# Cross-attention and mixture of experts: weighted sums of eight heads at a time, the projection in two halves

## The chip, the cores and the metric

One core of a Trainium2 chip. The time is that of one execution of the kernel on the device, in microseconds; less is better. Three runs of the kernel before took 1474.66, 1475.11 and 1478.47 us, median 1475.11 us.

## What is computed

The input is `x` of 32 batches of 112 tokens with 256 channels, and a context of 32 x 375 rows with 192 channels. One layer of cross-attention with 16 heads of 64, then a layer of 8 experts of which each token takes 2:

```python
q = (x @ Wq).reshape(b, lq, H, DK).transpose(0, 2, 1, 3)           # x after a layernorm
kv = (y @ Wkv).reshape(b, lkv, 2, H, DK).transpose(2, 0, 3, 1, 4)
atten = softmax(einsum('bhid,bhjd->bhij', q, k) * SCALE)
out = einsum('bhij,bhjd->bhid', atten, v) ... @ Wproj + bproj       # x = x + out
hidden = silu(gate_out) * up_out                                    # x after a second layernorm
output = sum of the two chosen experts' hidden @ down_w, by their gate shares   # x = x + output
```

## The kernel before, in words

Everything is one program in which each engine has its own list of instructions, written out by hand, and semaphores between them. TensorE (PE), VectorE (DVE), ScalarE (ACT), GpSimd (POOL) and SyncE (SP) each go through their list in order. First comes attention, then the experts (63 tiles of 128 rows). The change is in attention.

Attention runs in **pairs** of batches (`pair(i)`, 16 of them, `odd` = 0 and 1 within a pair), each batch in four **steps** (`s` = 0 to 3) of four heads. In a step PE does, in this order:

- the scores of four heads into the four PSUM banks `S_ps` (`scores`, L1521);
- products for the batch ahead: two blocks of K, begun by a short pair of 64-row products (`tails`, L1493, then `context_product`, L1486);
- an item "early" from the table `ahead`: a q product (L1429) or the transposes of `xn` (L1447);
- transposes of the probabilities of two heads (`turn_prob`, L1531), a V product (L1486), an item "mid", transposes of the other two heads, a second V product, an item "late";
- the weighted sums of the step's four heads into `O_ps` (`weigh`, L1555), and the tails of the two V products (L1493).

In step 2 there are no V products. There the projection of the batch before (`project`, L1576, 24 matmuls into `A_ps[1]`) stands between the K products and the transposes, and the small products that count tokens per expert (`count`, L1585) before the weighted sums.

Around it, ACT takes the exponentials (L891), the high parts of K, q and xT out of PSUM (L847 to L851), the transposed probabilities of heads 2 and 3 (`turned`, L897), at the end of step 0 four sums over the experts' gate products (`sum_experts`, L903), and one V block (L845). DVE takes the row maxima (`most`, L1279), the low parts (L1046), the transposed probabilities of heads 0 and 1 (L1285), the residual and its mean and variance (`residual`, L1125 to L1132, in step 2), the ranks of tokens in experts (`assign`, L1199 to L1207, in step 2) and the other V block (L1036). POOL normalises x2 (`norm_h`, L745 to L753) and splits the attention's result for the projection (`split_O`, L710).

A V block and a K block can share a bank: V's half 1, tile 1 (made in step 0, taken out by ACT at the step's end) lies in `A_ps[0]`, and so does the first K block of step 1. PE waits for a bank in `free_bank`, before the tails of K:

```python
for k in of_K:
    free_bank(a, k)
...
tails(a, of_K, True)
```

The last pair (`i == NP - 1`) is written out apart. Its gate logits go over PE: `turn_hn` (L1593) transposes the normalised rows of the batch before, which needs POOL's `hn`.

Of the kernel before, what the change touches and what calls it, by code (L numbers as in the profile page):

```python
# [65 lines left out]
PLACES = ("K", "early", "mid", "V", "late")  # L66


def ahead(odd, s):

    q_at = {(1, 0): (0,), (1, 1): (1,), (1, 2): (2, 3), (1, 3): (4,), (0, 0): (5,), (0, 1): (6,), (0, 2): (7,)}.get((odd, s), ())
    one = [("q", p) for p in q_at] + {(0, 2): [("xT", 0)], (0, 3): [("xT", 1)]}.get((odd, s), [])
    places = {"K": [("K", 2 * s), ("K", 2 * s + 1)],
              "early": one if s < 2 else [],
              "mid": one[:1] if s >= 2 else [],
              "V": [("V", t) for t in {0: ((1, 1), (1, 2)), 1: ((0, 0), (0, 1)), 3: ((0, 2), (1, 0))}.get(s, ())],
              "late": one[1:] if s >= 2 else []}
    return [(odd, s, place, kind, a) for place in PLACES for kind, a in places[place]]  # L80

# [20 lines left out]
def bank_of(items, k):  # L102
# [7 lines left out]
    return {"early": 1, "mid": 0 if s == 2 else 7, "late": 1}[place]  # L110
# [90 lines left out]

def dram_at(t, b):

    return t[b] if known(b) else t[bass.ds(b, 1)].rearrange("o q c -> (o q) c")


def attention_and_experts(nc, x, ctx_in, Wq, Wkv, Wproj, bproj, gate_w, gate_up_w, down_w, out):
# [4 lines left out]
    with ExitStack() as stack:  # L212
# [40 lines left out]
        gw_rows = nc.alloc_sbuf_tensor_at("gw_rows", [LQ, C, E], F32, offset=wgu_at + E * C * 4)  # L253
        weighed = nc.alloc_sbuf_tensor_at("weighed", [LQ, 2, C], F32, offset=wgu_at + E * C * 4)
        multiplied = nc.alloc_sbuf_tensor_at("multiplied", [LQ, E // 2, C], F32, offset=wgu_at + E * C * 4 + 2 * C * 4)
        logits = nc.alloc_sbuf_tensor_at("logits", [LQ, E], F32, offset=wgu_at + E * C * 4 + (2 + E // 2) * C * 4)
        assert 2 * E * C * 4 <= shared_from - wgu_at
# [14 lines left out]
        probT = sb("probT", [KR, 4, KT * LQ], F32)  # L272
# [57 lines left out]
        early = 2  # L330
        place["at"] = wd_at + early * FJ * C * 4
# [135 lines left out]
        def _(sp):  # L467
# [65 lines left out]
            def pair(i):  # L533
                a = Ahead(i)
                if known(i) and i == NP - 2:
                    sp.dma_start(Wd[:, 0:early].rearrange("p e k n -> p (e k) n"),
                                 down_w[0:early].rearrange("e (k p) n -> p (e k) n", p=P)).then_inc(wd_early, 16)
                for odd in (0, 1):
# [17 lines left out]
                    if known(i) and i == NP - 1 and not odd:  # L556
                        sp.wait_ge(gates_done, B - 3)
                        load_expert(sp, 0)
                    if known(i) and i == NP - 1 and odd:
# [274 lines left out]
        def _(act):  # L834
# [59 lines left out]
            def turned(b, s, j):  # L894

                act.wait_ge(probT_made, H * b + 4 * s + j + 1)
                nc.scalar.copy(probT[:, j, :], S_ps[j][0:KR, 0:KT * LQ]).then_inc(probT_second, 1)  # L897
# [19 lines left out]
            def pair(i):  # L917
                a = Ahead(i) if there(i, NP) else None
                for odd in (0, 1):
                    b = 2 * i + odd  # L920
                    for s in range(NS):
# [20 lines left out]
                        if there(b, B):  # L942
                            turned(b, s, 2)
                            turned(b, s, 3)
                        if s == 0 and there(b - 2, B) and by_vector(b - 2):
                            sum_experts(b - 2)
                        for k in made_at["late"]:
                            evacuate(a, k)
# [67 lines left out]
        def _(dve):  # L1016
# [102 lines left out]
            def residual(i, b, slot, bank):  # L1119
# [5 lines left out]
                nc.vector.tensor_tensor(x2[:, slot, :], bank[0:LQ, 0:C], x_bias[:, slot, :], ALU.add).then_inc(x2_done, 1)  # L1125
                dve.wait_ge(x2_done, b + 1)
# [155 lines left out]
            def turned(b, s, j):  # L1282

                dve.wait_ge(probT_made, H * b + 4 * s + j + 1)
                nc.vector.tensor_copy(probT[:, j, :], S_ps[j][0:KR, 0:KT * LQ]).then_inc(probT_first, 1)  # L1285

            def pair(i):
                a = Ahead(i) if there(i, NP) else None
                for odd in (0, 1):
                    b = 2 * i + odd  # L1290
                    for s in range(NS):
# [7 lines left out]
                        if s == 3 and there(b - 1, B) and not by_vector(b - 1):  # L1299
                            keep_hnT(b - 1, A_ps[1])  # L1300
# [480 lines left out]
```

## Time and profile before

| what | value |
|---|---|
| median of 3 runs | 1475.11 us |
| the profiled execution | 1475.41 us, of which its span 1473.6 us |
| PE busy | 1432.4 us (97%) |
| DVE, ACT, POOL busy | 1058.9 us (72%), 856.5 us (58%), 624.7 us (42%) |
| granted TensorE clock, mean | 0.992 |
| first scores of the first batch | 30.71 us |
| first scores of the last step | 1126.27 us |

Times in rows are counted from the first instruction. A PE row's duration is a modelled one with the latency in it; how long PE is held by a group is read from the start of one group to the start of the next. "Idle before" names what an engine waited for. In the order of instructions, register and ISA rows carry no work.

### The profile page before, as it was taken

The numbers are of one execution on the slowest core, as the hardware profiler recorded it, in microseconds if no ns is written. First come the engines' busy times: TensorE is split into PE (matmuls) and PEld (weight loads), VectorE is DVE, ScalarE is ACT, GpSimd is POOL, SyncE is SP. The second block draws the span as 40 slices with busy tenths as digits, with TensorE's granted clock in tenths as the row PEclk, the third lists the DMA queues.
The fourth block names the chain that finished last, engine by engine and source line by source line (L and its number), as shares of the span: only waits on it lengthen the run. The fifth ranks groups of instructions, "written<-read, shape, count | busy, mean of one in ns | idle before, by whom it ended". The sixth has DMA issues, their size and how long they took to land.

```text
span 1473.6 us, 38599 instructions
## 1 busy us (share of the span) xinstructions
PE 1432.4 (97%) x11960; PEld 1266.3 (86%) x11961; DVE 1058.9 (72%) x2868; ACT 856.5 (58%) x2392; POOL 624.7 (42%) x671
## 2 busy tenths in 40 slices
PE   6999999999999999999999999999997999999996
PEld 5888888888888888888888888888886788888885
DVE  5667777777777777777777777777768776666664
ACT  5566556555665566656655655556655555555553
POOL 2634344344545343545344443545436242333332
PEclk9999999999999999999999999999998899999998
DMA  9322222222222222322222222212128233333332
GB/s 262 108 68 69 75 73 74 67 76 67 73 67 73 73 80 78 94 82 68 73 67 73 74 73 70 73 38 73 28 64 314 50 66 56 55 52 57 51 57 26
DMA packets 101508, 114.75 MB, mean 78 GB/s; under 512 B 17276, under 2 KB 88172, under 8 KB 101356
## 3 DMA queue, kind: packets, MB, share of 16 engines
q1 hardware_dynamic: 88300, 95.25, 22.0%
q0 software_dynamic: 12144, 15.66, 5.9%
q10 hardware_dynamic: 1024, 3.34, 0.7%
q8 instruction: 21, 0.34, 0.1%
q14 instruction: 19, 0.16, 0.0%
HBM read 62.28 MB, written 51.93 MB: 78 GB/s over the span
## 4 chain that ended last, share of the span: by engine, by line
PE 87%; DVE 6%; DMA 3%; issue 2%; ACT 2%; DVEq 0%; ACTq 0%; POOLq 0%; SPq 0%
PE bank L1486 23%; PE bank L1429 22%; PE bank L1555 11%; PE bank L1531 10%; PE bank L1521 8%; PE bank L1576 6%; PE bank L1493 4%; DVE neg_max L1279 2%; DMA out<-y_out,dest_now 2%; PE bank L1731 2%; ACT prob L891 1%; DVE probT L1285 1%; PE bank L1684 1%; DVE Wgu L1138 1%; DMA WkU_whole<-in_L_xattn_Wkv 0%
## 5 line engine op out<-in xcount | busy, mean ns | idle before, releaser
L891 ACT ACTIVATE prob<-bank,neg_max 112x375 f32<-112x375 f32 x512 | 299.0, 589 | 133.7 <-DVE neg_max L1279 133.7
L1279 DVE TENSOR_REDUCE neg_max<-bank 112x1 f32<-112x375 f32 x512 | 244.0, 540 | 14.5 <-PE bank L1521 14.4
L1531 PE MATMUL bank<-ident,prob 112*125 112x112 f32 x1536 | 216.5, 273 | 6.5 <-ACT prob L891 2.4
L1531 PEld LDWEIGHTS bank<-ident,prob 112*125 112x125 f32 x1536 | 197.7, 188 | 20.0 <-ACT prob L891 14.0
L822 POOL DMA_INDIRECT out<-y_out,dest_now x63 | 97.8, 1553 | 200.4 <-DMA out<-y_out,dest_now 144.4
L1555 PEld LDWEIGHTS bank<-probT,V 125*64 125x64 f32 x3072 | 149.1, 137 | 39.0 <-issue 36.5
L1046 DVE TENSOR_TENSOR K_l<-bank,K_h 128x376 fp32r<-128x376 f32 x256 | 140.5, 550 | 56.9 <-ACT K_h L847 52.7
L1555 PE MATMUL bank<-probT,V 125*64 125x112 f32 x3072 | 176.6, 264 | 2.7 <-DVE probT L1285 1.9
L1429 PE MATMUL bank<-Wgu,hT_h 128*128 x504 | 166.6, 412 | 2.3 <-DVE hT_l L1347 2.2
L845 ACT COPY V<-bank 125x512 f32<-125x512 f32 x96 | 56.5, 588 | 164.3 <-PE bank L1493 161.7
L847 ACT CAST K_h<-bank 128x376 fp32r<-128x376 f32 x256 | 121.0, 473 | 31.7 <-PE bank L1486 29.4
L710 POOL CAST OT_h<-O_now 128x448 fp32r<-128x448 f32 x64 | 37.5, 586 | 213.1 <-DVE O_now L1115 213.1
L745 POOL TENSOR_SCALAR std<-mv 112x1 f32<-112x1 f32 x32 | 7.7, 240 | 281.9 <-DVE mv L1132 281.9
L1285 DVE COPY probT<-bank 125x336 f32<-125x336 f32 x256 | 121.3, 495 | 0.1
L897 ACT COPY probT<-bank 125x336 f32<-125x336 f32 x256 | 100.3, 443 | 27.4 <-PE bank L1531 27.0
L1486 PE MATMUL bank<-yA_h,WkH 128*128 128x376 f32 x256 | 99.6, 389 | 12.3 <-DVE WkU L1064 12.3
L1036 DVE COPY V<-bank 125x512 f32<-125x512 f32 x96 | 66.4, 692 | 62.0 <-PE bank L1493 55.5
L1429 PEld LDWEIGHTS bank<-Wgu,hT_h 128*128 128x128 f32 x504 | 91.0, 191 | 22.4 <-issue 5.3
L1008 ACT ACTIVATE y_out<-bank,share_now 128x256 f32<-128x256 f32 x63 | 29.9, 475 | 137.4 <-PE bank L1429 137.4
L891 ACT ACTIVATION_READ_ACCUMULATOR prob<-bank,neg_max 112x1 f32 x512 | 108.1, 211 | 0.0
L1429 PE MATMUL bank<-Wgu,hT_l 128*128 x252 | 100.1, 397 | 0.0
L849 ACT CAST q_h<-bank 128x224 fp32r<-128x224 f32 x128 | 45.4, 355 | 85.6 <-PE bank L1429 85.6
(217 smaller groups left out, 4008.9 us busy)
## 6 DMA issues: line engine op xcount, KB each, us to landing
bins<-pad_rows SPq DMA_DIRECT2D x29, 1032.0 KB, 5.9
inv_rows<-sums SPq DMA_DIRECT2D x126, 128.0 KB, 2.9
h_in<-bins SPq DMA_DIRECT2D x63, 129.0 KB, 2.3
Wgu<-in_L_ffn_gate_up_w SPq DMA_DIRECT2D x6, 1024.0 KB, 7.0
y_sb<-in_ctx SPq DMA_DIRECT2D x32, 187.5 KB, 2.7
y_sb<-in_ctx SPq DMA_DIRECT2D x62, 93.8 KB, 2.7
x_sb<-in_x SPq DMA_DIRECT2D x16, 224.0 KB, 3.0
x_res<-in_x SPq DMA_DIRECT2D x32, 112.0 KB, 2.4
```

Source lines behind the costliest of these rows:

```text
L822: pool.indirect_dma_start(out, bass.IndirectOffsetOnAxis(ap=dest_now[:, (k + 3) % 4:(k + 3) % 4 + 1], axis=0), y_out[:, (k + 1) % 2, :], N ...
L847: nc.scalar.copy(K_h[:, arg, :], src[:, 0:LKE]).then_inc(hi_done, 1)
L891: nc.scalar.activation(prob[:, j, :], S_ps[j][0:LQ, 0:LKV], ACT.Exp, bias=neg_max[:, j:j + 1], accum_out=row_sum[:, head // HB, head % HB: ...
L897: nc.scalar.copy(probT[:, j, :], S_ps[j][0:KR, 0:KT * LQ]).then_inc(probT_second, 1)
L1046: nc.vector.tensor_tensor(lo, ps, hi.bitcast(F32), ALU.subtract).then_inc(lo_done, 1)
L1279: nc.vector.tensor_reduce(neg_max[:, j:j + 1], S_ps[j][0:LQ, 0:LKV], AX.X, ALU.max, negate=True).then_inc(max_done, 1)
L1285: nc.vector.tensor_copy(probT[:, j, :], S_ps[j][0:KR, 0:KT * LQ]).then_inc(probT_first, 1)
L1429: last = mm(dst, w, m, start=n == 0, stop=n == len(todo) - 1)
L1486: last = mm(out, w, y, start=begins and n == 0, stop=ends and n == "both")
L1521: last = mm(S_ps[2 * k + r][0:LQ, 0:LKE], w[rows, p, q], m[rows, p, :], start=n == 0, stop=n == len(todo) - 1)
L1531: last = nc.tensor.transpose(S_ps[j][0:KR, t * LQ:t * LQ + LQ], prob[:, j, t * KR:t * KR + KR], ident[0:LQ, 0:LQ])
L1555: last = mm(O_ps[r * DK:r * DK + DK, c:c + LQ], V[:, t, (2 * p + r) * DK:(2 * p + r) * DK + DK], probT[:, 2 * k + r, t * LQ:t * LQ + LQ], ...
```

## The change

- `weigh` runs only at the end of steps 1 and 3, for eight heads, in all pairs but the last (`merged`). The transposed probabilities of even and odd steps go to two tiles; `probT_odd` lies where four small tiles were, which move to the room of the first experts' down weights, and those weights' load moves into the last pair.
- Scores of steps 1 and 3 get waits of their own for the transposed probabilities to be out of `S_ps`.
- The projection's first half stays before the first transposes of step 2, the second half goes behind the second transposes.
- `residual` loses its mean and variance, which go to step 3 behind the low parts of K (`moments`); the residual itself goes behind the transposed probabilities and the item "mid".
- The place "late" goes away. Items: q0 and q1 in step 0 of the odd batch, q2 in its step 1, q3 in step 2 (mid), q4 in step 3 (early), q5 and q6 in step 0 of the even batch, q7 in its step 1; xT of step 2 in "mid", of step 3 in "early".
- In the last pair `turn_hn` stands behind the second transposes of step 3.

```diff
-    q_at = {(1, 0): (0,), (1, 1): (1,), (1, 2): (2, 3), (1, 3): (4,), (0, 0): (5,), (0, 1): (6,), (0, 2): (7,)}.get((odd, s), ())
+    q_at = {(1, 0): (0, 1), (1, 1): (2,), (1, 2): (3,), (1, 3): (4,), (0, 0): (5, 6), (0, 1): (7,)}.get((odd, s), ())
...
+def merged(i):
+
+    return not known(i) or i < NP - 1
...
                     if known(i) and i == NP - 1 and not odd:
                         sp.wait_ge(gates_done, B - 3)
+                        sp.wait_ge(pv_made, NS * (B - 2))
                         load_expert(sp, 0)
+                        sp.dma_start(Wd[:, 0:early].rearrange("p e k n -> p (e k) n"),
...
-            def turned(b, s, j):
+            def turned(b, s, j, to):
...
                 nc.vector.tensor_tensor(x2[:, slot, :], bank[0:LQ, 0:C], x_bias[:, slot, :], ALU.add).then_inc(x2_done, 1)
+
+            def moments(b, slot):
+
                 dve.wait_ge(x2_done, b + 1)
                 nc.vector.bn_stats(stat2[:], x2[:, slot, :]).then_inc(st2, 1)
...
+                        if s == 3 and there(b - 1, B):
+                            moments(b - 1, 1 - odd)
                         if s == 2 and there(b, B):
                             normalise(b, 0)
-                        if s == 2 and there(b - 1, B):
-                            residual(i, b - 1, 1 - odd, A_ps[1])
...
                         for k in made_at["mid"]:
                             low_part(a, k)
+                        if s == 2 and there(b - 1, B):
+                            residual(i, b - 1, 1 - odd, A_ps[1])
...
+                    if s % 2 and merged(b // 2 if known(b) else b):
+                        pe.wait_ge(probT_second if k else probT_first, 2 * NS * b + 2 * s)
...
-                            project(b - 1, A_ps[1])
-                        if s == 3 and there(b - 1, B) and not by_vector(b - 1):
-                            for k in a.at(odd, 2, "late") if a else []:
-                                pe.wait_ge(lo_done, a.split(k))
-                            turn_hn(b - 1, 1 - odd, A_ps[1])
+                            project(b - 1, A_ps[1], (0,))
...
                             turn_prob(b, s, 1)
+                        if s == 2 and there(b - 1, B):
+                            project(b - 1, A_ps[1], (1,))
+                        if s == 3 and there(b - 1, B) and not by_vector(b - 1):
+                            turn_hn(b - 1, 1 - odd, A_ps[1])
...
-                        if there(b, B):
-                            weigh(a, odd, s, b)
+                        if there(b, B) and not merged(i):
+                            weigh(a, odd, s, b, probT[0])
+                        if there(b, B) and merged(i) and s % 2:
+                            weigh(a, odd, s - 1, b, probT[0])
+                            weigh(a, odd, s, b, probT[1])
```

How it moves instructions, at three places. PE at the end of step 1, even batch of the repeated pair (L1555 and L1568 are the weighted sums, the rows with `WvU,yT` the tails of V); before, then changed:

```order
L1486 MATMUL bank<-WvL,yA_h 125x512
L1486 MATMUL bank<-WvT,yB 125x512
L1551 REGISTER_ALU
L1555 MATMUL bank<-probT,V 64x112 x12
L1493 MATMUL bank<-WvU,yT 125x512 x2
```

```order
L1497 MATMUL bank<-WvT,yB 125x512
L1552 REGISTER_ALU
L1556 REGISTER_ALU
L1568 MATMUL bank<-probT,V 64x112 x12
L1564 REGISTER_ALU
L1568 MATMUL bank<-probT_odd,V 64x112 x12
L1504 MATMUL bank<-WvU,yT 125x512 x2
```

Two groups of twelve now stand together, and the end of step 0 has none.

ACT in step 0 of the same batch, from the K blocks' high parts on; before, then changed:

```order
L849 CAST q_h<-bank 128x224
L890 REGISTER_ALU
L891 ACTIVATE prob,row_sum<-bank,neg_max 112x375
L897 COPY probT<-bank 125x336 x2
L901 REGISTER_ALU
L903 ACTIVATE multiplied,logits<-multiplied 112x256 x4
L841 REGISTER_ALU
L845 COPY V<-bank 125x512
```

```order
L856 CAST q_h<-bank 128x224
L897 REGISTER_ALU
L898 ACTIVATE prob,row_sum<-bank,neg_max 112x375
L848 REGISTER_ALU
L856 CAST q_h<-bank 128x224
L904 COPY probT<-bank 125x336 x2
L908 REGISTER_ALU
L910 ACTIVATE multiplied,logits<-multiplied 112x256 x4
L848 REGISTER_ALU
L852 COPY V<-bank 125x512
```

A second q block is taken out ahead of the transposed probabilities; the four sums and the V block keep their order behind them.

DVE in step 2 of the same batch, from the low parts of K on; before, then changed:

```order
L1115 TENSOR_TENSOR O_now<-bank,inv_rows 128x448
L1124 REGISTER_ALU
L1125 TENSOR_TENSOR x_115<-bank,x_bias 112x256
L1127 BN_STATS stat_117<-x_115 112x6
L1132 BN_AGGR mv_118<-stat_117 112x2
L1285 COPY probT<-bank 125x336 x2
L1038 REGISTER_ALU
L1046 TENSOR_TENSOR q_l<-bank,q_h 128x224
L1038 REGISTER_ALU
L1046 TENSOR_TENSOR xT_l<-bank,xT_h 128x2x112
L1199 TENSOR_TENSOR bin_at<-bank,running 112x8
```

```order
L1121 TENSOR_TENSOR O_now<-bank,inv_rows 128x448
L1294 COPY probT<-bank 125x336 x2
L1044 REGISTER_ALU
L1052 TENSOR_TENSOR xT_l<-bank,xT_h 128x2x112
L1130 REGISTER_ALU
L1131 TENSOR_TENSOR x_112<-bank,x_bias 112x256
L1208 TENSOR_TENSOR bin_at<-bank,running 112x8
L1210 TENSOR_TENSOR running<-bank,running 128x8
L1211 TENSOR_TENSOR picked<-onehot,bin_at 112x16
```

The residual now stands between the last low part and the ranks, directly ahead of step 3's maxima.

## Rows read from the trace of the kernel before

**Rows 1.** One pair (us; PE, PEld, DVE, ACT, POOL busy; clock; DMA share; GB/s).

```profile
653.76:723.16 69.40, 69.09 (x630) 61.32 (x628) 52.22 (x155) 41.73 (x130) 31.34 (x36) 1.00 0.24 74
```

**Rows 2.** PE timeline, step 0 into 1 (start, duration, engine, line, out<-in, count).

```profile
658.78 0.81 PE L1531 MATMUL bank<-ident,prob 112*125 112x112 f32 x6
659.36 0.48 PE L1486 MATMUL bank<-WvH,yA_h 128*125 128x512 f32 x1
660.45 1.37 PE L1555 MATMUL bank<-probT,V 125*64 125x112 f32 x24
661.75 0.49 PE L1493 MATMUL bank<-WvU,yT 64*125 64x512 f32 x2
663.10 0.35 PE L1493 MATMUL bank<-yT,WkU 64*128 64x376 f32 x2
```

**Rows 3.** Chain of waits from 600 us on: a piece of one weighted-sum group.

```profile
599.99 0.77 PE bank L1555 x16
```

**Rows 4.** ACT timeline, end of the same step 0.

```profile
661.48 0.20 ACT L903 ACTIVATION_READ_ACCUMULATOR multiplied<-multiplied 112x1 f32 x1
662.28 0.59 ACT L845 COPY V<-bank 125x512 f32<-125x512 f32 x1 [0.61 <-PE bank L1493]
```

**Rows 5.** One transpose after a wait (timeline); the group's mean (page).

```profile
648.43 0.36 PE L1531 MATMUL bank<-ident,prob 112*125 112x112 f32 x1
L1531 PE MATMUL bank<-ident,prob 112*125 112x112 f32 x1536 | 216.5, 273 | 6.5 <-ACT prob L891 2.4
```

**Rows 6.** PE timeline, step 3 of the same batch.

```profile
679.72 0.42 PE L1521 MATMUL bank<-K_h,q_h 64*112 64x376 f32 x2
682.57 1.20 PE L1531 MATMUL bank<-ident,prob 112*125 112x112 f32 x6
683.53 0.47 PE L1486 MATMUL bank<-WvH,yA_h 128*125 128x512 f32 x1
```

**Rows 7.** DVE timeline, end of step 2 into step 3.

```profile
676.31 0.42 DVE L1125 TENSOR_TENSOR x<-bank,x_bias 112x256 f32<-112x256 f32 x1 [1.09 <-PE bank L1576]
676.76 0.43 DVE L1127 BATCH_NORM_STATS2 stat<-x 112x6 f32<-112x256 f32 x1
679.23 0.16 DVE L1199 TENSOR_TENSOR bin_at<-bank,running 112x8 f32<-112x8 f32 x1
680.51 1.91 DVE L1279 TENSOR_REDUCE neg_max<-bank 112x1 f32<-112x375 f32 x4 [0.45 <-PE bank L1521]
683.53 0.55 DVE L1046 TENSOR_TENSOR K_l<-bank,K_h 128x376 fp32r<-128x376 f32 x1 [0.38 <-ACT K_h L847]
```

**Rows 8.** PE timeline, end of step 2: token counts, then the weighted sums.

```profile
678.18 0.17 PE L1585 MATMUL bank<-chosen,before 112*112 112x8 bf16 x1
678.41 1.18 PE L1555 MATMUL bank<-probT,V 125*64 125x112 f32 x20
```

**Rows 9.** ACT timeline, step 3.

```profile
681.10 0.58 ACT L891 ACTIVATE prob<-bank,neg_max 112x375 f32<-112x375 f32 x1 [2.21 <-DVE neg_max L1279]
682.09 0.47 ACT L847 CAST K_h<-bank 128x376 fp32r<-128x376 f32 x1 [0.33 <-PE bank L1486]
682.46 0.58 ACT L891 ACTIVATE prob<-bank,neg_max 112x375 f32<-112x375 f32 x1
```

**Rows 10.** POOL timeline, the normalised rows of that batch.

```profile
678.84 2.44 POOL L753 TENSOR_SCALAR hn<-x,mv,std 112x256 f32<-112x256 f32 x2 [0.20 <-POOL std L747]
```

**Rows 11.** Last step of all, PE and DVE timelines.

```profile
1126.27 0.43 PE L1521 MATMUL bank<-K_h,q_h 64*112 64x376 f32 x2
1131.52 2.51 PE L1555 MATMUL bank<-probT,V 125*64 125x112 f32 x24
1127.14 1.91 DVE L1279 TENSOR_REDUCE neg_max<-bank 112x1 f32<-112x375 f32 x4
```

**Rows 12.** Busy time by stretch, last pair.

```profile
1096.23:1126.27 30.04, 26.50 (x257) 22.65 (x256) 20.25 (x58) 18.29 (x47) 23.31 (x18) 1.00 0.55 188
1131.30:1138.00 6.70, 6.30 (x42) 5.49 (x40) 5.93 (x11) 2.16 (x3) 2.85 (x2) 0.50 1.03 407
```

More of the change, by code:

```diff
@@ L58 @@
 N2 = NT - N1
-PLACES = ("K", "early", "mid", "V", "late")
+PLACES = ("K", "early", "mid", "V")
 def ahead(odd, s):
-    q_at = {(1, 0): (0,), (1, 1): (1,), (1, 2): (2, 3), (1, 3): (4,), (0, 0): (5,), (0, 1): (6,), (0, 2): (7,)}.get((odd, s), ())
-    one = [("q", p) for p in q_at] + {(0, 2): [("xT", 0)], (0, 3): [("xT", 1)]}.get((odd, s), [])
+    q_at = {(1, 0): (0, 1), (1, 1): (2,), (1, 2): (3,), (1, 3): (4,), (0, 0): (5, 6), (0, 1): (7,)}.get((odd, s), ())
+    ones = [("q", p) for p in q_at] + {(0, 2): [("xT", 0)], (0, 3): [("xT", 1)]}.get((odd, s), [])
     places = {"K": [("K", 2 * s), ("K", 2 * s + 1)],
[L76 to L79, printed above, removed]
+              "early": ones[:1] if s != 2 else [],
+              "mid": ones[1:] if s != 2 else ones,
+              "V": [("V", t) for t in {0: ((1, 1), (1, 2)), 1: ((0, 0), (0, 1)), 3: ((0, 2), (1, 0))}.get(s, ())]}
     return [(odd, s, place, kind, a) for place in PLACES for kind, a in places[place]]
@@ L109, in bank_of @@
         return int(a in SECOND)
-    return {"early": 1, "mid": 0 if s == 2 else 7, "late": 1}[place]
+    return {"early": 1, "mid": 0 if s == 2 else 7}[place]
 class Ahead:
@@ L330, in attention_and_experts @@
         early = 2
+        gw_rows = nc.alloc_sbuf_tensor_at("gw_rows", [LQ, C, E], F32, offset=wd_at)
+        place["at"] = wd_at
+        weighed = sb("weighed", [LQ, 2, C], F32)
+        multiplied = sb("multiplied", [LQ, E // 2, C], F32)
+        logits = sb("logits", [LQ, E], F32)
+        assert place["at"] <= wd_at + early * FJ * C * 4 and E <= early * FJ
         place["at"] = wd_at + early * FJ * C * 4
@@ L942, in pair @@
                         if there(b, B):
-                            turned(b, s, 2)
-                            turned(b, s, 3)
+                            to = probT[s % 2 if merged(i) else 0]
+                            turned(b, s, 2, to)
+                            turned(b, s, 3, to)
                         if s == 0 and there(b - 2, B) and by_vector(b - 2):
                             sum_experts(b - 2)
-                        for k in made_at["late"]:
-                            evacuate(a, k)
                         if known(b) and b == B - 1 and s == 3:
@@ L1533, in turn_prob, with weigh @@
                     last.then_inc(probT_made, 1)
-            def weigh(a, odd, s, b):
+            def weigh(a, odd, s, b, weights):
                 if s == 0:
@@ L1556, in weigh @@
                                       V[:, t, (2 * p + r) * DK:(2 * p + r) * DK + DK],
-                                      probT[:, 2 * k + r, t * LQ:t * LQ + LQ], start=t == 0, stop=t == KT - 1)
+                                      weights[:, 2 * k + r, t * LQ:t * LQ + LQ], start=t == 0, stop=t == KT - 1)
                 last.then_inc(pv_made, 1)
@@ L1566, in turn_last_inverses, with project @@
                 last.then_inc(inv_turned, 1)
-            def project(b, bank):
+            def project(b, bank, halves=range(2)):
                 if known(b) and b == 0:
                     pe.wait_ge(wp_done, 8)
-                for half in range(2):
+                for half in halves:
                     pe.wait_ge(OT_lo, 2 * b + half + 1)
@@ L1577, in project @@
                                       stop=j == NJ - 1 and n == 2)
-                last.then_inc(proj_made, 1)
+                if 1 in halves:
+                    last.then_inc(proj_made, 1)
             def count(b):
@@ L1625, in pair @@
                         for k in early:
+                            if s == 3 and there(b - 1, B):
+                                pe.wait_ge(x2_done, b)
                             make(a, k, i)
@@ L1645, in pair @@
                             turn_prob(b, s, 1)
+                        if s == 2 and there(b - 1, B):
+                            project(b - 1, A_ps[1], (1,))
+                        if s == 3 and there(b - 1, B) and not by_vector(b - 1):
+                            turn_hn(b - 1, 1 - odd, A_ps[1])
                         for k in of_V[1:]:
@@ L1652, in pair @@
                             context_product(a, k, True, False)
-                        for k in made_at["late"]:
-                            if there(b - 1, B):
-                                pe.wait_ge(x2_done, b)
-                            make(a, k, i)
                         if s == 0 and there(b - 2, B) and not by_vector(b - 2):
```

33 lines of the change are left out of this document (13 added, 20 removed).

## Prediction

> **What bounds the kernel now.** I read the busy shares first: PE is busy 97% of the span. So the second view is one pair by itself, and there PE is busy 69.09 of 69.40 us at a granted clock of 1.00 [rows 1]. A pair costs what PE's list costs, plus the few places where PE waits. That made the PE timeline the third view: where is an interval from one group to the next longer than the same group's elsewhere? Then the timelines of DVE and ACT around those places, and those of the last pair. Only three kinds of terms can matter: PE time that the new order saves, waits that go, and waits that come. 14 pairs are alike; the first and the last are counted apart.
>
> **Weighted sums merged.** A group of 24 PE instructions holds PE from 660.45 to 661.75, 1.30 us [rows 2]. Inside a group 16 of them take 0.77 us [rows 3], so 24 alone would take 1.155. The other 0.145 us is paid at the group's edges, where PE changes from one division of its array to another. The change joins 8 groups of a pair into 4: 4 x 0.145 = **0.58 us saved a pair**. Other edges stay: V's tails (64 rows) follow a 128-row product instead of the sums, which is a change of division too.
>
> **Step 2's end.** In the even batch the counts stand at 678.18 and the sums start at 678.41 [rows 8], 0.23 us for two matmuls that together hold PE about 0.12; the sums waited for DVE's transposed probabilities. They are no longer there to wait: **0.12 saved**. The new waits of the scores of steps 1 and 3 cost nothing: between the last transposes and the second pair of scores lie V product and tails (1.09 + 0.33 us) or the projection's second half (about 1.4), and ACT needs 0.5 + 2 x 0.35. Without that cover each would cost up to 1 us.
>
> **Step 1, a new wait.** In step 0 ACT goes through transposed probabilities, four expert sums, then the V block. From the second transposes at 658.78 the last sum is read out at 661.48, 2.70 us later [rows 4]. The V copy now starts only at 662.28 because it waits for V's tails, lands 0.59 us later, and PE needs its bank at 663.10, for the K tails of step 1 [rows 2, 4]: a margin of 0.2 us. In the change 1.30 us of weighted sums is gone from between. PE comes to the K tails 663.10 - 658.78 - 1.30 = 3.02 us after the transposes. ACT is no faster: the copy can start at 2.70 + 0.1, lands at 3.39, and is seen a few hundredths later. The second q product stands ahead of the transposes and moves both alike. **PE waits about 0.41 us**, and the first matmul after a wait shows 0.36 against a mean of 0.273 [rows 5], 0.09 more. That is 0.5 us a batch, **1.0 a pair**. DVE is late here as well (its count of the top gates waits for the same sums, and V copy and maxima stand behind it: some 0.8 us), but PE stands still 0.5 of that and ACT's wait for the K products takes up the rest.
>
> The Trainium skill (TensorE: Matmul & The Clock Gate, "Step-by-step: what each phase is for") says that TensorE pulls weight loads ahead of matmuls in flight. By that a restart would cost nothing, and the sum would be 4 x 0.09 a pair, some 5 us in all, lower. The trace sides with the cost: the lone transpose above. I keep 0.09.
>
> **Step 3, the old wait.** Transposes begin at 682.57 and the V product at 683.53, 0.96 us [rows 6], against 0.58 in step 0 [rows 2]: PE waits 0.38 us for the second head's exponentials, in each batch. The change puts a q product (0.66 us, as in step 0) ahead of them in the odd batch and two xT transposes (0.19) in the even one. But DVE now comes later. Its maxima start 0.79 us after the scores (679.72 to 680.51), waiting only for PE. In the change the residual waits for the projection's second half, directly before the scores: it starts some 0.2 us after them (a matmul's latency of 0.3 less the counts' 0.1, an estimate), then 0.45 to the ranks (676.31 to 676.76), then 0.83 (679.23 to 680.51 less 0.45 idle) [rows 7]. So the maxima start about 1.45 us in, 0.65 later. ACT takes up most of it, since it idled 0.33 before the first K copy [rows 9]: the second exponential, now 2.74 us in, comes at 2.85 to 2.95. The odd batch is covered at the first transposes; at the second, with the q copy in ACT's list before the last exponential, about 0.1 us is left: 0.38 becomes 0.1, **0.28 saved**. The even batch has 0.19 us of cover against 0.38 plus 0.15, and 0.2 to 0.3 at the second transposes (the xT copy now stands before the last exponential): 0.38 becomes 0.55, **0.17 lost**.
>
> **What costs nothing.** Mean and variance move to step 3: DVE is busy 52 of 69 us [rows 1], and the work behind them (transposed probabilities) has the sums of step 2's heads as cover, 1.2 us. POOL's norm starts some 4 us later; it is busy 31 of 69 us. If that cover were gone, the gate products would delay DVE's V copy at the next step 0. Later O_now in step 0, later split: the projection is 10 us away. The loads of down weights queue on SP behind expert 0 and are wanted after attention. Without cover that would be up to 6 us, once.
>
> **A pair:** -0.58 - 0.12 + 1.0 + 0.17 - 0.28 = **+0.19 us**; 14 of them +2.7. The first pair has no expert sums, so no wait in step 1: -0.8.
>
> **The last pair.** It keeps groups of four heads, so it saves no edges. (a) Batch 30, step 3: `turn_hn` needs POOL's rows. Mean and variance now follow the second low part of K, which starts at 3.8 us in (683.53 - 679.72) and takes about 0.5. From their start to the first half of `hn` it is 678.84 - 676.76 = 2.1, plus half of 2.44 [rows 7, 10]: ready at about 7.7 us. PE arrives at 5.5 (scores 1.1, K 1.7, transposes 0.96, V 1.0, transposes 0.6). It waits 2.2 us, and the V product then waits 0.6 for DVE to copy the result; with more at the transposes: +3.2. (b) In step 2 of batches 30 and 31 the second half projection covers what PE waited for: -1.3. (c) Last step: the maxima start 0.87 us in [rows 11]. Residual, ranks and the five steps of the plan (2.4 us) follow the projection, from which the scores are only 1.3 us of sums away: maxima at about 1.75. Then mean and variance, 3.3 us to `hn`, transposes, copy, and the inverse sums behind them on DVE: the weighted sums start about 9 us in, against 1131.52 - 1126.27 = 5.25 [rows 11]. +3.7, and what follows up to the first experts hangs on it. Together **+5.6 us**.
>
> **Sum:** 2.7 - 0.8 + 5.6 = +7.5 us. The profiled execution was 1475.4 us (span 1473.6), as good as the median of 1475.1. **Forecast: 1483 us.**
>
> **Bounds.** The wait in step 1, by the copy's own margin, is at least 0.3 and, if the read-out must end first, 0.6 with restart and late DVE 0.8: -0.4 to +0.6 a pair, -6 to +8 us. A 128-row product directly before V's tails is not in the rows inside a pair; its edge could be nothing or the 0.145: -0.3 to +0.3 a pair. The last pair: 2 (PE busy elsewhere hides half) to 8.
>
> **Rivals.** (1) *Waits outweigh the edges mildly*, the forecast: 1479.5 to 1487. For it: the margin of 0.2 us in step 1 against 1.3 removed. Chance 0.60. (2) *ACT is in time.* If the V copy lands before PE is 3.02 us past the transposes, the edges remain: pair -0.8, 15 x -0.8 + 5.6 = -6.4, so **1469**. It decides at a copy done 0.4 us sooner than its row allows. Against it: ACT's four sums run without a gap. Chance 0.09. (3) *The last pair is cheap*: POOL and DVE chains overlap with waits that exist already, +2 rather than +5.6, and the pairs near zero: **1477**, no change. Chance 0.12. (4) *The end turns slow.* The granted clock was 1.00 from 1096 to 1126 us with PE busy 26.5 of 30 us, and 0.50, the 1.2 GHz level, from 1131.3 to 1138.0 after step ends full of waits [rows 12]. More waits begin at batch 30's step 3 already. One more such stretch of 6.7 us at half speed gives away up to 3.4, two about 5, and step-1 waits of 0.6 add 5: **1489**. Chance 0.19.
>
> The Trainium skill (same page, "The HAM clock gate") has TensorE fall back to half rate after idling; by that rule (4) would gain weight. The trace agrees as to the fall at 1131.3, but shows none at the waits of the last pair before.
>
> That the merge does not take place is ruled out by the order of instructions.
>
> **Numbers.** 0.3%, 4.4 us, is about what a measurement can tell from no change. Slower by more: (1) and (4), 0.79. Same: (3), 0.12. Faster: (2), 0.09. The range leaves out (2) and the far end of (4): 1476 to 1491.
>
> **What would show it.** A pair of 69.4 to 69.8 us; groups of 48 instructions of 2.45 us; before the K tails of step 1 a gap of 0.4 us ended by ACT's V copy; transposes of step 3 at 0.58 in the odd and about 0.7 in the even batch; in batch 30 over 2 us of PE waiting for `hn`. The prediction is wrong if step 1 shows no gap, or if the last scores of attention start less than 3 us later than 1126.27.

## The result: slower by 1.0%

| | before | changed |
|---|---|---|
| median of 5 runs each | 1476.74 us | 1492.03 us |
| ratio | | 1.0101 (95% interval 1.0086 to 1.0117) |
| span of the profiled execution | 1473.6 us | 1489.7 us |
| a pair of batches | 69.40 us | 69.90 us |
| from the last pair's first scores to the end | 403.4 us | 412.2 us |

The forecast was 1483.0 us (1476 to 1491): the sign was right, the size half of what came. Of 16.1 us between the two spans, 14 pairs bring 7.0 (forecast 2.7), the last pair and the end 8.7 (forecast 5.6), the first pair -0.3 (forecast -0.8); the rest is a first score 0.7 us later. Two executions, one of the kernel before with 4788.1 us and one of the kernel with pieces (below) with 2751.6 us, are left out of all medians and ratios as slow ones.

The pair that answers to [rows 1], and its first two steps (busy time by stretch; PE, PEld, DVE, ACT, POOL; clock):

```profile
658.16:728.06 69.90, 69.29 (x632) 61.56 (x629) 53.27 (x155) 41.10 (x130) 31.72 (x37) 1.00 0.25 74
658.16:665.85 7.69, 7.69 (x59) 6.76 (x57) 5.78 (x14) 5.84 (x20) 5.72 (x5) 1.00 0.79 239
665.85:675.89 10.04, 9.74 (x102) 8.38 (x100) 7.17 (x28) 5.64 (x20) 5.40 (x9) 1.00 0.16 45
```

Step 0 has no wait. Step 1 has one of 0.30 us in every batch, and it is the one forecast. PE and ACT timelines around it, as in [rows 2, 4]:

```profile
663.83 0.81 PE L1544 MATMUL bank<-ident,prob 112*125 112x112 f32 x6
666.71 0.33 PE L1534 MATMUL bank<-K_h,q_l 64*112 64x376 f32 x2
667.33 0.44 PE L1504 MATMUL bank<-yT,WkU 64*128 64x376 f32 x2 [0.30 <-ACT V L852]
...
666.54 0.19 ACT L910 ACTIVATION_READ_ACCUMULATOR multiplied<-multiplied 112x1 f32 x1
666.63 0.57 ACT L852 COPY V<-bank 125x512 f32<-125x512 f32 x1
```

From the second transposes (663.83) to the last sum's read-out (666.54) it is 2.71 us, as before. The V copy follows at once, lands at 667.20, and PE starts the K tails at 667.33. "Idle 0.30" is less than PE loses, since the modelled ends of the matmuls in flight cover part of it. By starts it is more: over the 12 pairs in the middle, scores and K tails of step 1 take 1.86 us in either batch, where before they took 1.30. That is 0.56 us a batch.

Step 3 of the same even batch, the rows that answer to [rows 6, 7, 9]:

```profile
686.16 1.04 PE L1544 MATMUL bank<-ident,prob 112*125 112x112 f32 x6
687.99 0.94 PE L1544 MATMUL bank<-ident,prob 112*125 112x112 f32 x6
683.27 0.42 DVE L1131 TENSOR_TENSOR x<-bank,x_bias 112x256 f32<-112x256 f32 x1 [1.40 <-PE bank L1589]
684.39 1.91 DVE L1288 TENSOR_REDUCE neg_max<-bank 112x1 f32<-112x375 f32 x4
685.89 0.58 ACT L898 ACTIVATE prob<-bank,neg_max 112x375 f32<-112x375 f32 x1
```

The scores began at 683.10. The residual starts 0.17 us behind them (forecast 0.2), the maxima 1.29 (forecast 1.45), the second exponential 2.79 (forecast 2.85 to 2.95). The first transposes wait 0.23 us, the second 0.38; averaged over the pairs, transposes and V products of this step take 0.26 us more in the even batch and 0.24 less in the odd one.

The last pair. PE timeline of batch 30's step 3, then POOL and DVE around the start of batch 31's step 2:

```profile
1111.03 0.38 PE L1607 MATMUL bank<-ident,hn 112*128 112x112 f32 x2 [2.13 <-POOL hn L760]
1109.65 2.44 POOL L760 TENSOR_SCALAR hn<-x,mv,std 112x256 f32<-112x256 f32 x2 [0.20 <-issue]
1107.56 0.42 DVE L1136 BATCH_NORM_STATS2 stat<-x 112x6 f32<-112x256 f32 x1
...
1127.18 4.57 POOL L699 TENSOR_TENSOR Wgu<-Wgu 128x2048 fp32r<-128x2048 f32 x1
1128.55 3.24 DVE L1188 CAST top_f<-top_i 112x2 f32<-112x2 uint32 x1
```

The 2.13 us for `hn` are the forecast 2.2. The last two rows were not foreseen. DVE's cast of the chosen experts' numbers, two to a row, takes 3.24 us, where its median over the kernel is 0.17, and it ends at 1131.79 us; POOL's subtraction, the low part of an expert's weights, ends at 1131.75. In the kernel before the same pair of rows stands there, but the cast takes only 1.18 us, since POOL's subtraction ended 2 us earlier against the step (0.25 us behind its first scores, now 2.30):

```profile
1113.40 4.53 POOL L692 TENSOR_TENSOR Wgu<-Wgu 128x2048 fp32r<-128x2048 f32 x1
1116.78 1.18 DVE L1179 CAST top_f<-top_i 112x2 f32<-112x2 uint32 x1
```

Behind the cast stand the maxima, the exponentials and PE: step 2 of batch 31 takes 10.64 us, before 8.59. What PE and DVE do there, first the kernel before (its scores at 1117.68), then the changed one (scores at 1129.45):

```profile
1118.56 1.91 DVE L1279 TENSOR_REDUCE neg_max<-bank 112x1 f32<-112x375 f32 x4
1124.97 1.37 PE L1555 MATMUL bank<-probT,V 125*64 125x112 f32 x24 [1.66 <-DVE probT L1285]
```

```profile
1132.38 1.91 DVE L1288 TENSOR_REDUCE neg_max<-bank 112x1 f32<-112x375 f32 x4
1133.67 2.42 PE L1544 MATMUL bank<-ident,prob 112*125 112x112 f32 x12 [1.34 <-ACT prob L898]
```

The wait of 1.66 us ahead of the sums has gone. But the maxima start 2.93 us behind the scores instead of 0.88, so that PE waits ahead of and between the transposes. On top of that the second half projection takes 2.68 us, in batch 30 1.49: the granted clock is 0.50, the 1.2 GHz level, from 1135.6 to 1139.0.

### The profile page after: what moved, and what is told of

The parts are those of the page before. It is cut to its first block and busy times, and to the rows that moved or that the text cites. A ratio compares the mean times of both kernels' runs of the same rounds, so it can differ in the third digit from the quotient of the medians.

```text
span 1489.7 us, 38675 instructions
## 1 busy us (share of the span) xinstructions
PE 1436.0 (96%) x11960; PEld 1270.2 (85%) x11961; DVE 1076.3 (72%) x2868; ACT 847.3 (57%) x2392; POOL 631.4 (42%) x671
## 5 line engine op out<-in xcount | busy, mean ns | idle before, releaser
L1568 PEld LDWEIGHTS bank<-probT,V 125*64 125x64 f32 x1632 | 80.3, 139 | 23.9 <-issue 23.4
L1568 PE MATMUL bank<-probT,V 125*64 125x112 f32 x1632 | 95.1, 267 | 0.0
L1497 PE MATMUL bank<-WvH,yA_h 128*125 128x512 f32 x192 | 91.9, 479 | 0.9 <-DVE hnT L1153 0.6
L1534 PE MATMUL bank<-K_h,q_h 64*112 64x376 f32 x512 | 88.7, 342 | 0.3 <-DVE probT L1294 0.3
L1497 PE MATMUL bank<-yA_l,WkH 128*128 128x376 f32 x256 | 86.4, 337 | 0.0
L1497 PE MATMUL bank<-yB,WkT 128*128 128x376 f32 x256 | 86.2, 337 | 0.0
```

The source lines that it names most:

```text
L1497: last = mm(out, w, y, start=begins and n == 0, stop=ends and n == "both")
L1534: last = mm(S_ps[2 * k + r][0:LQ, 0:LKE], w[rows, p, q], m[rows, p, :], start=n == 0, stop=n == len(todo) - 1)
L1568: last = mm(O_ps[r * DK:r * DK + DK, c:c + LQ], V[:, t, (2 * p + r) * DK:(2 * p + r) * DK + DK], weights[:, 2 * k + r, t * LQ:t * LQ + LQ] ...
```

## The experiments

Twelve runs followed. The first four (the three marked first, and the sums twice) ran in a session in which the kernel before took 1483.9 us instead of 1476.7, so three of them ran once more in a later one, in which it took 1475.2; the record gives the chip the number 2 both times. The ratio is always to the kernel before in the same session. "End" is the time from the last pair's first scores to the end of the span.

| kernel | time | ratio, interval | pair | end |
|---|---|---|---|---|
| the changed kernel again (c_after) | 1492.6 | 1.0112 (1.0097, 1.0127) | 69.89 | 414.4 |
| the kernel before again, one execution (c_before) | 1475.1 | | 69.40 | 402.2 |
| sums early, first (e1) | 1482.4 | 0.999 (0.998, 1.000) | 69.2 | 414.2 |
| sums early, second (c_sums_early) | 1475.6 | 0.9999 (0.9989, 1.0009) | 68.79 | 413.5 |
| sums twice (e2) | 1512.4 | 1.0184 (1.0165, 1.0204) | 72.0 | 407.7 |
| last pair old, first (e3) | 1492.1 | 1.0051 (1.0033, 1.0069) | 70.65 | 403.3 |
| last pair old, second (c_last_pair_old) | 1484.0 | 1.0052 (1.0035, 1.007) | 69.90 | 405.1 |
| unmerged, first (e4) | 1494.6 | 1.0066 (1.0044, 1.0088) | 70.13 | 411.5 |
| unmerged, second (c_unmerged) | 1497.7 | 1.0147 (1.013, 1.0164) | 70.11 | 412.9 |
| moments of the last pair early (e10) | 1486.1 | 1.0064 (1.0047, 1.008) | 69.89 | 406.3 |
| POOL's split in pieces (e8) | 1492.0 | 1.0118 (1.01, 1.0136) | 69.90 | 411.7 |
| both cures (e5) | 1467.9 | 0.9947 (0.9935, 0.9959) | 68.75 | 403.7 |

### Step 1: take the wait away, and make it without the change

Sums early, on the changed kernel, in ACT's step 0:

```diff
+                        if s == 0 and there(b - 2, B) and by_vector(b - 2):
+                            sum_experts(b - 2, 0, 2)
                         for k in made_at["mid"]:
                             evacuate(a, k)
...
-                            sum_experts(b - 2)
+                            sum_experts(b - 2, 2, 4)
```

> The changed kernel, but in step 0 ACT takes two of its four expert sums ahead of the q copy (the item mid) instead of all four at the step's end. Theory (the loss inside a pair is PE's wait at step 1 for ACT's V copy, which stands behind the four sums): the copy comes some 0.8 us sooner, the wait of 0.56 us a batch goes, step 1 falls from 10.04 to about 9.5 us in both batches, a pair from 69.90 to 68.7 to 69.0 us, and the time from 1492.0 by 13 to 17 us to 1475 to 1479. Rival 1 (step 1 is longer since the joined groups change the array's division before V's tails, or since the scores wait for the transposed probabilities): step 1 stays at 10.0 us, the time at 1492. Rival 2 (the two sums ahead of the q copy make that copy and so the last exponentials late): the wait moves to step 0's second transposes, a pair stays at 69.5 or above.

> The changed kernel with two of ACT's four expert sums ahead of the q copy, again, for the same reason. Without the slow handover: step 1 of 9.48, pairs of 68.75, and 1492.0 - 16 = 1476, level with the kernel before (ratio 0.998 to 1.002).

In the second run step 1 took 9.48 us, every pair but the first 68.74 to 68.81, and the time was level with the kernel before. So the wait of step 1 is worth 1.11 us a pair, 15.5 us in all, as much as the whole difference between the two kernels: without it step 1 takes what it took before plus the 1.15 us of the moved sums. ACT has the room: it idled 0.82 us before the second q copy. With both cures the same place reads:

```profile
654.58 0.45 ACT L916 ACTIVATE multiplied<-multiplied 112x256 f32<-112x256 f32 x1
655.54 0.35 ACT L861 CAST q_h<-bank 128x224 fp32r<-128x224 f32 x1
657.55 0.59 ACT L857 COPY V<-bank 125x512 f32<-125x512 f32 x1
...
658.38 0.33 PE L1517 MATMUL bank<-yT,WkU 64*128 64x376 f32 x2
```

The sums stand ahead of the q copy, the V copy starts 0.20 us after PE's scores (657.35), and the tails have no wait and no dearer restart: 0.27 us from their start to the next group's, against 0.37.

Sums twice, on the kernel before, at the end of ACT's step 0:

```diff
+                for e in range(E // 2):
+                    nc.scalar.activation(multiplied[:, e, :], multiplied[:, e, :], ACT.Copy,
+                                         accum_out=logits[:, E // 2 + e:E // 2 + e + 1]).then_inc(more_sums, 1)
+                act.wait_ge(more_sums, 4 * b + 4)
                 for e in range(E // 2):
```

> The kernel before, unmerged, but ACT takes each of the four expert sums twice (four more readings of 0.40 us at the end of step 0, and a wait between the two sets). Nothing else moves. Theory (the V copy behind the sums has a margin of 0.2 us before PE misses its bank, and it idles 0.8 us before it can start): 1.7 us more make the copy 0.9 us later and PE waits 0.7 to 0.9 us before the K tails of step 1 in both batches; step 1 rises from 8.33 to 9.0 to 9.3, a pair from 69.40 to 70.8 to 71.3, the time from 1476.7 by 20 to 28 us. Rival (ACT has room, and what the changed kernel loses in step 1 comes from PE's own order): the pair stays within 0.3 us of 69.40 and the time within 4 us.

```profile
683.85 0.56 ACT L846 COPY V<-bank 125x512 f32<-125x512 f32 x1
684.54 0.43 PE L1498 MATMUL bank<-yT,WkU 64*128 64x376 f32 x2 [0.74 <-ACT V L846]
```

Step 1 rose from 8.33 to 9.33 in both batches, slightly over the forecast. The pair's other 0.56 us, which take it to 72.0 against a forecast of 70.8 to 71.3, stand in step 0 of the odd batch, where the slow handover below stands too. The wait comes with neither merged sums nor a new order, from ACT's list alone, so the rival is gone. What the merge did was to take 1.30 us of PE work from between.

### Is the merge itself worth its edges?

```diff
 def merged(i):
-    return not known(i) or i < NP - 1
+    return False
```

> The changed kernel with the weighted sums at the end of every step, in groups of four heads, in all pairs. All else stays changed. Theory (merging saves 0.60 us a pair at the groups' edges and brings the wait at step 1, 1.13 a pair): steps 0 and 2 rise by 1.30, steps 1 falls to 8.3 to 8.4 and step 3 by 1.15 to 1.2; a pair from 69.90 to 69.2 to 69.6 us, the time falls from 1492.0 by 4 to 10 us, to 1482 to 1488. Rival (the joined groups are worth their edges and the loss in step 1 comes from elsewhere, as the new order of q products): a pair rises by 0.6 to 70.5 and the time to 1500.

> The changed kernel unmerged, again, for the same reason. Without the slow handover, theory: the transposes of step 0 wait 0.2 to 0.3 us (its first run had 0.33, and 0.21 in the last pair, where no slow handover stood), edges cost 0.60, step 1 saves 1.13: pairs of 69.4 to 69.9 us against 69.90, time 1485 to 1492. If step 0 keeps 9.5 and 9.3 us, that wait belongs to the order and not to the chip, and merging is worth more than its edges.

Step 1 fell to 8.33, as the theory has it, and the edges came back (two groups at 1.301 us where one of 48 has 2.451). But the pair rose to 70.13 and 70.11 in the two runs: the transposes of step 0 wait 0.33 us in the even and 0.30 in the odd batch, and the even batch loses 0.18 more behind its second V product. These waits stand in both sessions and belong to the order, then. DVE's timeline shows where it comes from (scores of step 0 at 661.72):

```profile
660.93 0.64 DVE L1163 CUSTOM_DVE_ANT_0 weighed<-hn,gw_wide 112x256 f32<-112x256 f32 x1 [0.22 <-POOL hn L760]
662.89 0.68 DVE L1042 COPY V<-bank 125x512 f32<-125x512 f32 x1
663.49 1.90 DVE L1288 TENSOR_REDUCE neg_max<-bank 112x1 f32<-112x375 f32 x4
```

The gate products wait for POOL's `hn`, late by the mean and variance in step 3, and push V copy and maxima: 1.77 us after the scores, where the kernel before had them at 0.84 (654.60 after 653.76):

```profile
653.99 0.69 DVE L1036 COPY V<-bank 125x512 f32<-125x512 f32 x1
654.60 1.90 DVE L1279 TENSOR_REDUCE neg_max<-bank 112x1 f32<-112x375 f32 x4
```

So my expectation was wrong: in this order the long group at the end of step 3 hides the late `hn`, and merging is worth 0.2 us a pair even with its wait in step 1. (By ratio it is worth 5 to 7 us in all; the pairs account for 3.5 of them, 14 x 0.21 and 0.6 in the first.) The first run's lower ratio (1.0066) says nothing else: there the kernel before was 8.7 us slower and this one 3 us faster than in the second.

### The last pair

Last pair old, on the changed kernel (in `most`; PE's list accordingly: `project` whole, `turn_hn` ahead of the transposes):

```diff
+                        if s == 3 and last_pair(i) and not by_vector(b - 1):
+                            keep_hnT(b - 1, A_ps[1])
...
+                        if s == 2 and last_pair(i):
+                            residual(i, b - 1, 1 - odd, A_ps[1])
+                            moments(b - 1, 1 - odd)
```

> The changed kernel with the last pair in the order of the kernel before: the whole projection before the first transposes of step 2, residual, mean and variance together in step 2, and the transposes of hn ahead of the first transposes of step 3. Theory (moving mean and variance to step 3 makes hn late there, which costs 4.7 us in batch 30's step 3, 2 us in batch 31's step 2, where DVE's small cast stands 3.2 us beside POOL's expert split, and 2 us in the last step): the scores of the last step come 58 to 59 us after the last pair's first scores instead of 62.5, and the time falls by 5 to 9 us to 1483 to 1487. Rival (the last pair is slow for another reason: the new load of down weights, or half-clock stretches that come by themselves): the time falls by less than 2.5 us.

> The changed kernel with the last pair in the old order, again, since the first run of it had the slow handover in step 0 from the second pair on. Without it: pairs of 69.90, 402 to 404 us from the last pair's first scores to the end, time 1492.0 - 9 = 1483. If the first run was right (the cure is worth nothing), 1490 or more.

The end fell from 412.2 and 414.4 us to 403.3 and 405.1, against 403.4 and 402.2 of the kernel before. The cast is back at 1.38 and 1.09 us. By ratio (1.0052 against 1.0101 and 1.0112) the time is 7 to 9 us under the changed kernel's, as expected. The load of the down weights still stands in the last pair there, so it costs at most what is left of the end, 3 us, against the "up to 6" of a load without cover.

Which part of it? Only the moments of the last pair back in step 2:

```diff
+                        if s == 2 and last_pair(i):
+                            moments(b - 1, 1 - odd)
```

> The changed kernel, only with the mean and variance of the last pair directly behind the residual in step 2 (the two halves of the projection and the late transposes of hn stay). Theory (of the last pair's loss the larger part is the mean and variance in step 3, which make hn, and with it POOL's expert split, late): batch 30's step 3 falls from 11.4 (all of it at full clock) to 8.1 to 8.5 us, the hold of DVE beside POOL's split comes 2 us earlier or goes, and the time falls by 4 to 8 us. Rival (the halves of the projection and the place of the transposes cost it): the time falls by less than 2 us.

Batch 30's step 3 took 9.13 us against 11.44 at full clock (c_after), the cast 1.90, step 2 of batch 31 8.00 (10.64 and 11.62), the end 406.3, the time by ratio 5.5 to 7 us less. The mean and variance are the larger part. The kernel's PE timeline shows what is left:

```profile
1110.66 0.35 PE L1614 MATMUL bank<-ident,hn 112*128 112x112 f32 x2
1111.60 0.47 PE L1504 MATMUL bank<-WvH,yA_h 128*125 128x512 f32 x1 [0.58 <-DVE hnT L1158]
```

The transposes of `hn` no longer wait, but the V product behind them still waits 0.58 us for the bank to be read, the price of the new place of `turn_hn` (forecast 0.6). I had expected 8.1 to 8.5, without this.

### Does DVE stand still because POOL works?

On the changed kernel, POOL's `lo_of_expert`:

```diff
+                for piece in range(4):
+                    lo = Wgu[:, e, 1][:, :, piece * 256:piece * 256 + 256]
+                    hi = Wgu[:, e, 0][:, :, piece * 256:piece * 256 + 256]
+                    last = pool.tensor_tensor(lo, lo.bitcast(F32), hi.bitcast(F32), ALU.subtract)
```

> The changed kernel, but POOL forms the low part of experts 0 and 1 in four pieces of 512 columns instead of one operation of 4.57 us. Theory (DVE's cast of the chosen experts' numbers in batch 31's step 2 stands 3.24 us because it can't get through while POOL's two-input operation runs, and ends with it): the cast is held only to the end of a piece, at most 1.2 us, and step 2 of batch 31 falls from 10.6 us by 1.5 to 2.5, the time by 1 to 3 us. Rival (the cast is slow for a reason of its own, its operands or a wait that the trace hides): it stays above 3 us. Second rival (the lock is kept over POOL's whole run of operations): the cast stays at 3.2 us too, and ends with the last piece.

The changed kernel again, then the pieces; POOL and DVE around the start of batch 31's step 2:

```profile
1125.89 4.58 POOL L699 TENSOR_TENSOR Wgu<-Wgu 128x2048 fp32r<-128x2048 f32 x1
1125.82 0.17 DVE L1188 CAST top_f<-top_i 112x2 f32<-112x2 uint32 x1
1126.02 4.48 DVE L1191 TENSOR_TENSOR onehot<-iota_e,top_f 112x16 f32<-112x16 f32 x1
```

```profile
1127.16 5.00 POOL L702 TENSOR_TENSOR Wgu<-Wgu 128x512 fp32r<-128x512 f32 x4
1129.26 0.43 DVE L1191 CAST top_f<-top_i 112x2 f32<-112x2 uint32 x1
1129.72 1.22 DVE L1194 TENSOR_TENSOR onehot<-iota_e,top_f 112x16 f32<-112x16 f32 x1
1130.98 1.21 DVE L1200 TENSOR_TENSOR chosen<-onehot 112x8 bf16<-112x8 f32 x1
```

In the second profile of the changed kernel the cast came just ahead of POOL's operation and took 0.17 us; the comparison behind it took 4.48 and ended with POOL's. With pieces three instructions of DVE are held, none longer than a piece. So it is no property of the cast: certain DVE operations can't get through while POOL's subtraction runs, and MAX8, the reciprocal and the small reduction between them can.

The pieces cured nothing, though. The three short holds add up to the one long: POOL's split starts at 1127.16 and the maxima at 1132.38, in the changed kernel at 1127.18 and 1132.38. Step 2 of batch 31 fell to 8.43 us, inside the forecast, but for two other reasons. It began 0.74 us later against the split, since batch 30's step 3 took 13.9 us, part of it at half clock; and it had no half clock itself (second half projection 1.49 us, not 2.68). The time did not fall either (1.0118 against 1.0112).

### The control runs, and a slow handover

> The kernel before, unchanged, with a profile, beside the others. In the four runs so far the kernel before took 1483.9 us, not 1476.7, and two changed kernels show a handover of 0.75 us instead of 0.20 in step 0 (ACT's second q copy stands until 0.75 us after the end of the q product), from the second pair on. If that is a property of the chip in those runs, the kernel before shows it too: pairs of 69.9 to 70.0 us instead of 69.40. If this chip is as the first, 69.40.

> The changed kernel, unchanged, timed beside the others. Expected: ratio 1.010 to the kernel before. If the slow handover is the chip's, its pairs are 70.6 us as in the kernel with the old last pair, and its time 1500 where before takes 1484; if it belongs to single programs, its pairs stay at 69.90.

Neither showed it: pairs of 69.40 and 69.89. In the session of the first four, three kernels did. ACT's second q copy of step 0, the last pair old, first run:

```profile
458.97 0.35 ACT L861 CAST q_h<-bank 128x224 fp32r<-128x224 f32 x1 [1.40 <-PE bank L1450]
```

PE's next group began at 458.20, so it starts 0.77 us behind the q product; in the changed kernel, same pair, it is 0.20 (454.36, idle 0.82). In this kernel it is so in the even batches of pairs 2 to 11, and now and then in the odd ones; the kernel with the sums early had the same; in the sums-twice kernel V copies of both DVE and ACT started 0.69 to 0.78 us after the scores of the odd batch's step 0 instead of 0.20 to 0.23. The wait is for PE's semaphore each time. Whether PE was late where the trace models its ends, or the signal was, the trace doesn't tell, and why the unmerged kernel had none is open. The three that ran again later, on a chip of the same number, had none either, so it went with the session; whether a chip, its state or something else in that session made it isn't shown. There is no profile of the kernel before from that session.

### Both cures

> The changed kernel with both cures: two of ACT's four expert sums ahead of the q copy in step 0, and the last pair in the old order. Theory (the two losses are apart): a pair of 68.8 us where no slow handover stands in it, the last pair and the end as before (403 us from the last pair's first scores), together 1492.0 - 15.4 - 8.8 = 1468, against before 1476.7 a ratio of 0.993 to 0.995, 7 to 10 us faster than before. Rival (the gains overlap, since a faster pair only shifts the waits): the ratio stays at 0.999 as with the first cure alone.

1467.9 us, ratio 0.9947 (0.9935 to 0.9959): by ratio 7.8 us faster than the kernel before and some 24 faster than the changed one, within a microsecond of the expected 1468. The two losses add up, and the idea of the change holds: nearly all of the pair is PE work now.

```profile
649.66:718.41 68.75, 68.73 (x632) 61.48 (x628) 53.41 (x155) 41.55 (x130) 31.78 (x37) 1.00 0.25 75
657.35:666.84 9.49, 9.49 (x102) 8.39 (x99) 7.24 (x28) 5.09 (x17) 5.42 (x9) 1.00 0.18 49
```

## Why the prediction had the sign right and half the size

| term | forecast | measured |
|---|---|---|
| edges of the merged sums, a pair | -0.58 | -0.60 |
| end of step 2 | -0.12 | -0.11 |
| step 1, two batches | +1.0 | +1.12 |
| step 3, even | +0.17 | +0.26 |
| step 3, odd | -0.28 | -0.24 |
| the rest (projection's second half +0.14, q -0.17, K +0.04) | 0 | +0.07 |
| a pair | +0.19 | +0.50 |
| (a) batch 30, step 3 | +3.2 | +3.3 at full clock, +4.7 in the first profile |
| (b) batch 30, step 2, with the q product moved to step 0 | -1.3 with batch 31 | -0.3 |
| (b) batch 31, step 2 | | +2.1 (+2.5 in the second profiles) |
| (c) last step on | +3.7 | +2.3 (+6.7 in the second profiles) |

**Inside a pair** every mechanism was right and the net came out too small, +0.19 us for +0.50, which is 4.3 of the 8.6 us that the forecast missed. It is a small net of large terms of both signs: 0.12 us too little at step 1, 0.09 and 0.04 at step 3, 0.07 elsewhere, nearly all to one side, and each times 14. In step 1 four hundredths stood in for what is 0.13 from the copy's end to PE's start, and the restart was 0.106 (K tails 0.371 against 0.265), not 0.09. In step 3 the second transposes wait 0.38 in the even batch, not 0.2 to 0.3. The projection's second half, split off, costs 0.08 us more than the first behind the transposes, a cost that I had not listed. The first pair gained 0.3 us and not 0.8: in its even batch, whose step 2 has no projection, the q product that left had covered a wait, and the second transposes rose from 0.81 to 1.47 us.

The Trainium skill's pull-ahead of weight loads (TensorE: Matmul & The Clock Gate, "Step-by-step: what each phase is for") was read as making the restart free; the 0.106 us that vanish again with the wait speak against using it for a group behind a wait. The sum held two such restarts a pair (0.18 us, 2.5 in all), not the four that the prediction took off.

**The last pair** is where a step failed; it and the end brought 8.7 us for 5.6. It is (b), "in step 2 of batches 30 and 31 the second half projection covers what PE waited for". For batch 30 it did (counts 0.42 to 0.12). In batch 31 it did too (1.86 to 0.17 us from the counts to the sums), and still the step grew by 2.1 us where -1.3 was forecast for both batches. The forecast put at nothing what comes ahead of the first transposes. The change, by the same late mean and variance that (a) counted, moved POOL's split onto DVE's work there, DVE was held, and the maxima came 2.05 us later; the half clock in the second half projection then cost 1.2 us more. I had read POOL's rows only for `hn`. (a) was right to 0.1 us. In (c) the way to the weighted sums is 10.0 us, forecast 9, before 5.25, but of its 4.7 us only 2.3 reach the end in the first profiles, 6.7 in the second. The half-clock stretches behind the last step's first scores are 17 us before and 10 changed in the first profiles, 7 and 24 in the second, so they go with the spread between 2.3 and 6.7; that they make all of it isn't shown.

**Rivals.** (2), ACT in time, fell with the row of the V copy. (3), the last pair cheap, fell with 412.2 and 414.4. (4) lay nearest with 1489, for a reason half right: step 1 did cost near its 0.6 a batch, but the half-clock stretches are no fixed price. (Its own parts, 3.4 or 5 and another 5 on 1483, make 1491 to 1493, not 1489; that this is nearer to 1492 would be luck, for in the first profiles half-clock time in all is 17 us before and 17 changed.) The kernel before has 6.8 and 10.1 us of them behind 1131.2 us in one profile and one of 6.8 in the other; the changed kernel has a piece of 3.4 already in batch 30's step 3 in one profile, and three more of 3.4 to 6.9 later; in the other none there, but later one of 3.5 and one of 23.8:

```profile
1131.20:1138.00 6.80, 6.41 (x43) 5.55 (x41) 6.00 (x12) 2.16 (x3) 2.85 (x2) 0.50 1.03 407
1141.50:1151.60 10.10, 8.59 (x26) 6.60 (x26) 9.23 (x11) 7.96 (x9) 0.00 (x0) 0.50 0.26 85
...
1111.80:1115.20 3.40, 3.21 (x18) 2.39 (x20) 0.37 (x3) 0.00 (x0) 3.00 (x4) 0.51 0.03 5
...
1143.50:1167.30 23.80, 16.69 (x77) 13.94 (x77) 19.96 (x27) 12.21 (x14) 11.60 (x8) 0.50 0.50 182
```

**"What costs nothing"** held for the pairs only as long as its cover: it named the gate products delaying DVE's V copy if the cover went, and the unmerged kernel shows just that.

## What to carry to other kernels

When work is merged or moved on the busiest engine, list for each bank what its reader does until then, for a margin of 0.2 us is gone once 1.3 us of cover leave; the cure was to move the reader's other work into an idle gap earlier in the same step. When a producer is moved later, follow its consumers through every engine's list up to the end of the program, also those that only share a resource with the engine on the path.

## What the runs showed of the hardware

- DVE's cast from and to SBUF, and its operations with two SBUF inputs, took 3.24 and 4.48 us instead of 0.17 and ended with POOL's two-input subtraction (4.57 and 4.58 us); with that cut in four, each was held for no more than one piece, but three in a row for as long in all. The Trainium skill (SBUF — State Buffer, "Who interferes with whom") says that a DVE instruction with two SBUF inputs contends with a GpSimd instruction that reads SBUF, and that a cast can too in a mode that uses two ports; they share a port pair, and the one that comes second is blocked. The trace agrees as to the holds; in which mode the cast ran no row shows.
- The K tails behind a wait cost 0.106 us more than without one (0.371 against 0.265), and a joined group of 48 saves 0.15 us against two of 24, in every pair alike.
- In one session ACT or DVE started 0.5 to 0.7 us later than usual behind a group of PE, at one place of a step, pair after pair, in some programs and not in others. The unmerged kernel had none of it, but came out at 1.0066 there and at 1.0147 later, so a ratio of one session can be off by 0.8%.
